# Moving ScalarE's copies of a turned layer step and of turned attention weights to other places of its row order

## The reference

```python
# layer 0
adj = adj + eye(N); d = sum(adj, -1) ** -0.5
out = (d[:, None] * adj * d[None, :]) @ x @ W.T + b
# layer 1
q, k = x @ WQ, x @ WK
h = relu(q[:, None, :, :] + k[:, :, None, :])          # for each pair (i, j)
score = einsum('bijd,d->bij', h, p)
out = softmax(score + where(adj > 0, 0, -1e22), -1) @ x
# layer 2 (degrees from |adj + eye|) and layer 3 (from adj)
out = (d[:, None] * adj * d[None, :]) @ x @ W + b
# after each layer
x = layernorm(x + out)
```

## Time and profile before

| | us |
|---|---|
| median of 3 runs | 14193.57 |
| lowest, highest | 14191.82, 14194.89 |
| the profiled execution's own time | 14193.55 |
| its span, first to last instruction | 14191.7 |
| PE busy | 13028.6 (92%) |
| VectorE busy | 13378.4 (94%) |
| ScalarE busy | 13088.8 (92%) |
| GpSimd busy | 908.8 (6%) |
| mean granted TensorE clock | 0.98 |

### The profile page before, as it was taken

The page is one execution under the profiler, slowest core; times in us unless marked ns, Lnnn a source line. Parts: engine busy times, 40 slices in busy tenths (PEclk is TensorE's granted clock), DMA queues, the critical chain, the costliest instruction groups (busy, mean ns, idle before and its releaser), DMA issues.

```text
span 14191.7 us, 317692 instructions
## 1 busy us (share of the span) xinstructions
PE 13028.6 (92%) x143877; PEld 5473.6 (39%) x143877; DVE 13378.4 (94%) x14048; ACT 13088.8 (92%) x8612; POOL 908.8 (6%) x615
## 2 busy tenths in 40 slices
PE   6889989999899998999989998899989999899988
PEld 3333334443344433443334433344333443333333
DVE  5999999999999999999999999999999999999995
ACT  5999899998999999998999989999899998998994
POOL 0000000000000000001000000000000010000000
PEclk8999999999999999999999999999999999999999
DMA  5111112221122111221122211222112221011103
GB/s 185 45 52 47 49 52 84 87 61 49 56 86 88 61 41 61 87 88 58 36 73 85 85 55 36 77 83 85 59 35 74 88 80 56 30 49 52 43 12 108
DMA packets 714329, 935.45 MB, mean 66 GB/s; under 512 B 61712, under 2 KB 455952, under 8 KB 693520
## 3 DMA queue, kind: packets, MB, share of 16 engines
q1 hardware_dynamic: 712976, 915.13, 20.6%
HBM read 722.01 MB, written 184.55 MB: 64 GB/s over the span
## 4 chain that ended last, share of the span: by engine, by line
PE 45%; DVE 31%; ACT 20%; issue 2%; DMA 2%; SPq 0%; POOL 0%; ACTq 0%; DVEq 0%; POOLq 0%
PE score L1165 33%; DVE big L1019 27%; ACT big L783 18%; PE acc L1086 6%; PE turn L1063 2%; PE acc L1145 2%; DVE att L968 1%; DVE gx L898 1%; DMA piece<-adj_turned 1%; DMA q_pair_kept<-turned 1%; PE acc L1104 1%; ACT y_turned L706 0%; ACT turned L696 0%; DVE stats L904 0%; DMA big<-in_adj_dram 0%
## 5 line engine op out<-in xcount | busy, mean ns | idle before, releaser
L1019 DVE TENSOR_SCALAR big<-q_pair,k_pair_cols 128x2048 f32<-128x2048 f32 x10120 | 12224.7, 1280 | 418.9 <-PE score L1165 400.1
L783 ACT ACTIVATE big<-q_f,k_cols 128x2048 f32<-128x2048 f32 x6144 | 11744.7, 1998 | 63.5 <-DMA q_f<-q_kept 43.3
L1165 PE MATMUL score<-big,sign_window 128*32 128x512 f32 x49152 | 5612.0, 597 | 291.4 <-ACT big L783 287.1
L1165 PE MATMUL score<-big,unit_window 128*32 128x512 f16 x81920 | 5186.5, 397 | 726.0 <-DVE big L1019 708.0
L1165 PEld LDWEIGHTS score<-big,unit_window 128*32 128x32 bf16 x81920 | 2285.8, 97 | 3897.8 <-issue 1110.4
L1165 PEld LDWEIGHTS score<-big,sign_window 128*32 128x32 f32 x49152 | 1565.3, 110 | 3624.9 <-issue 3002.2
L1086 PE MATMUL acc<-piece,gs 128*128 128x512 f32 x3072 | 1446.2, 598 | 34.8 <-DVE gs L881 22.4
L1086 PEld LDWEIGHTS acc<-piece,gs 128*128 128x128 f32 x3072 | 533.6, 191 | 544.6 <-issue 459.5
L607 POOL TENSOR_SCALAR att_var<-att_mom 128x1 f32<-128x1 f32 x128 | 66.2, 517 | 9806.9 <-DVE att_mom L986 9806.9
L764 ACT ACTIVATE att_turned<-turn 128x512 f32<-128x512 f32 x512 | 299.9, 586 | 346.2 <-PE turn L1063 346.0
L1145 PE MATMUL acc<-x,att_turned 128*128 128x128 f32 x4096 | 555.2, 279 | 0.0
(11 more groups left out here) (89 smaller groups left out, 2705.6 us busy)
## 6 DMA issues: line engine op xcount, KB each, us to landing
piece<-adj_turned SPq DMA_DIRECT2D x1536, 256.0 KB, 2.7
att<-in_adj_dram SPq DMA_DIRECT2D x128, 1024.0 KB, 5.2
raw<-in_adj_dram SPq DMA_DIRECT2D x224, 512.0 KB, 4.6
adj_turned<-turned SPq DMA_DIRECT2D x224, 512.0 KB, 4.3
big<-in_adj_dram SPq DMA_DIRECT2D x32, 512.0 KB, 7.5
adj_turned<-big SPq DMA_DIRECT2D x32, 512.0 KB, 6.9
gx<-in_x_dram SPq DMA_DIRECT2D x32, 256.0 KB, 4.4
q_kept<-raw SPq DMA_DIRECT2D x32, 256.0 KB, 3.7
```

The costliest lines, as they stand in the source:

```text
L783: ins = nc.scalar.activation(ring["A"][:, RANK[g] % RING * 4 + u, :], q_f32[:], ACT.Relu, bias=k_cols[:, t % 2, QUAD * u + g:QUAD * u + g ...
L1019: ins = nc.vector.tensor_scalar(ring["D"][:, RANK[g] % RING * 4 + u, :], q_pair[:], k_pair_cols[:, t % 2, QUAD * u + g:QUAD * u + g + 1], ...
L1165: ins = nc.tensor.matmul(score[QUAD * u:QUAD * (u + 1), cc, :], window[:, QUAD - 1 - g:2 * QUAD - 1 - g], row, start=(g == 0 and part == 0 ...
```

## The change

Two things move on ScalarE. The copy of a turned layer step goes from the side work of group 26 to that of group 28, which is ScalarE's work before the rows of group 29; it is then behind the rows of group 26 and behind the copy of a turned raw quarter at group 27. The constant TURNED_AT also enters the two places that work out which steps and passes lie before which others; no pass lies between 26 and 28. And the four copies of turned weights go from the start of groups 9, 13, 17 and 22, ahead of the side work there, to behind the first of the four rows of groups 10, 13, 18 and 23. The number of instructions, their shapes and all waits stay as they are.

```diff
-    SELF_AT, TURNED_AT, PROJECT_AT, SUM_AT, ROOT_AT, NORM_OUT_AT, STORE_AT = 18, 26, 28, 35, 36, 40, 41
+    SELF_AT, TURNED_AT, PROJECT_AT, SUM_AT, ROOT_AT, NORM_OUT_AT, STORE_AT = 18, 28, 28, 35, 36, 40, 41
...
-        COPY_AT = {9: 0, 13: 1, 17: 2, 22: 3}
+        COPY_IN = {10: 0, 13: 1, 18: 2, 23: 3}
...
-                    if before and g in COPY_AT:
-                        copy_weights(c * T + (T + t - 1), COPY_AT[g])
                     side(c, place)
                     if KIND[g] == "A":
...
                         for u in range(P // QUAD):
+                            if before and u == 1 and g in COPY_IN:
+                                copy_weights(c * T + (T + t - 1), COPY_IN[g])
                             ins = nc.scalar.activation(ring["A"][:, RANK[g] % RING * 4 + u, :], q_f32[:], ACT.Relu,
```

## The result

| us | kernel before | changed kernel |
|---|---|---|
| median | 14191.6 (12 runs) | 14158.08 (12 runs) |
| lowest, highest | 14181.26, 14204.43 | 14150.9, 14165.78 |
| profiled execution, its span | 14193.55, 14191.7 | 14165.78, 14164.0 |
| mean granted TensorE clock | 0.980 | 0.977 |

The ratio is 0.9976, with a 95% interval of 0.9967 to 0.9985: 33.5 us faster, where 34.2 had been forecast. The profiled execution of the changed kernel is the slowest of its 12.

The account below looks back on a forecast made before the run. TensorE, ScalarE and VectorE, passing work round a ring of two groups, were taken to bound the kernel together. 17.8 + 15.5 + 3.8 - 2.9 = 34.2 us off 14193.57 gave 14159.4, range 14136 to 14195.

Parts of the forecast that it names:

- Part 1, tied borders: Layer copy behind group 26: where VectorE's chain is only 0.60 us behind TensorE's, even-block borders gain 0.60 us before copy costs.
- borders 5 and 9: Behind blocks 5 and 9 VectorE is 1.0 and 1.3 us late by its own work: nothing to win.
- the whole stop: Rival: each of 84 borders gives TensorE's 1.13 us wait at group 26, 14099 us; chance 0.05.
- VectorE alone: Rival: VectorE alone sets the time, so the layer copy and queue give nothing, about 14195 us; chance 0.14.
- Part 2, what the copies cost: Weight copies inside groups: 0.48 us later from group 13, cutting some middle-batch border gains; +2.9 us in block 0.
- Block 0's 0.48: In block 0 of the six later batches ScalarE sets the pace from group 13; 0.48 us paid each, +2.9 us.
- No slower kernel from group 13: Denies the rival that ScalarE, late from group 13, paces blocks 3 to 8: 14218 or 14202 us; chance 0.09.
- the 0.2 named as the limit: Forecast is wrong if TensorE gets new waits before groups 13, 18 and 21 of more than 0.2 us.
- The stop of 0.20 us named for group 21 of block 6: With ScalarE's rows of group 21 later, TensorE is 0.20 us late there, and so is VectorE's group 27.
- A wait inside a group: Copies breaking up four like rows taken to cost nothing; if each of some 74 lost one overlap, 7 us worse.
- Part 3, the queue: Behind blocks 11 and 12 the query pair's store leaves 1.11 us sooner on SyncE's queue: 14 borders, 15.5 us.
- Odd blocks' wait at group 26: TensorE's wait for ScalarE's rows of group 26 would fall from 1.15 to about 0.9 us in odd blocks.

Follow-up runs that it names:

- corner 12: Changed kernel plus ten unused identity products on TensorE ahead of group 4's scores in blocks 3 to 13, holding its clock: 14090.64 us, ratio 0.9931.
- corner 9: Kernel before, neither copy moved, plus ten unused identity products ahead of group 4's scores in blocks 3 to 13: 14141.01 us, ratio 0.9967.
- corner 10: Kernel before with only the copies of turned weights moved, plus ten unused products ahead of group 4's scores in blocks 3 to 13: 14142.76 us, ratio 0.9968.
- run 6: Changed kernel with the second quarter's weight copy put back ahead of group 13's side work: 14162.26 us, ratio 0.998.
- 11: Kernel before with only the layer copy moved, plus ten unused products ahead of group 4's scores in blocks 3 to 13: 14092.83 us, ratio 0.9931.
- run 3: Changed kernel with the query pair's store on SyncE's queue at group 27 instead of 29, ahead of the piece loads: 14137.64 us, ratio 0.9961.

## Why the prediction came out, step by step

With the clock held the traces can be read border by border. Take the distance between TensorE's first scores of group 4 in one block and in the next, corner 12 less corner 9, mean of the six middle batches, against the steps of the forecast (us; the border is named by the block before it):

```
border      0     1     2     3     4     5     6     7     8     9    10    11    12    13    14    15
forecast  +.48    0   -.60  -.42  -.60    0   -.40  -.19  -.40    0   -.35 -1.11 -1.11    0     0     0
measured  +.47  -.39  -.50  -.47  -.59  +.01  -.45  -.19  -.48  -.03  -.36 -1.28 -1.32  -.53  +.14  -.38
spread     .05   .88   .31   .03   .08   .07   .05   .09   .03   .04   .11   .34   .59   .56   .69  1.07
```

The spread is the standard deviation over the six batches.

- **Part 1, tied borders.** Right, each within 0.10 us; borders 5 and 9, said to be VectorE's own, gave nothing. Neither the whole stop (-1.13 each) nor VectorE alone (0) fits this row of numbers. Forecast for the seven borders 2, 3, 4, 6, 7, 8 and 10: 2.96 a batch; measured 3.04.
- **Part 2, what the copies cost.** Block 0's 0.48 is there (+0.47; +0.46 in corner 10 alone). In corner 10 borders 3 to 8 are longer by 0.04 to 0.36; in the six middle batches all borders sum to +9.9 us, where about 8 followed from the forecast's steps. That the time does not show it lies outside these borders: in corner 10's profile the first and last batch are 5.2 us shorter together, and the scores begin 3.6 us earlier, in an opening without any such copy. Over the 12 profiles with the store at its old place that start varies by 6.5 us (237.6 to 244.1; 231.4 and 231.6 with the early store), so a single profile's opening proves nothing, and run 6, which took the largest of these costs away without a gain in time, leaves it open whether they reach the time.
- **No slower kernel from group 13.** Right: the new wait of TensorE in block 7 is 0.13 us at group 18, under the 0.2 named as the limit. The stop of 0.20 us named for group 21 of block 6 is recorded as no idle time, but TensorE's starts do shift by it: with the copies moved (corner 12 less 11) the scores behind group 21 come 0.22 us later, 0.07 of it at group 13.
- **A wait inside a group.** It cost no overlap: the row behind the copy at 7834.28 starts at 7834.75 (0.47 later), and the copy starts 1.90 behind the row before it. Over all 512 copies of the changed kernel the median of the first distance is 0.48 us, the same as before. ScalarE around block 6's group 10, changed kernel:

```profile
7832.38 2.01 ACT L783 ACTIVATE big<-q_f,k_cols 128x2048 f32<-128x2048 f32 x1
7834.28 0.59 ACT L764 ACTIVATE att_turned<-turn 128x512 f32<-128x512 f32 x1
7834.75 5.81 ACT L783 ACTIVATE big<-q_f,k_cols 128x2048 f32<-128x2048 f32 x3
```

- **Part 3, the queue.** Right in kind, low in size. VectorE arrives 1.33 us later in relation to TensorE's group 28 than before, not 1.11, and the store leaves 1.00 us behind that group's start in both. The mean of the 14 waits fell by 1.00 us in the first pair and by 1.34 with the clock held (2.11 to 0.78): 14 x 1.34 = 18.7 us against 15.5. From its issue until VectorE goes on the store takes 3.6 to 5.8 us, which is why single blocks, such as the one shown, can look unchanged.
- **Odd blocks' wait at group 26.** 0.58 to 0.68 us where I said about 0.9; where ScalarE gained the difference was not looked into.
- **The term that was missing.** Nothing in the sum stood for the clock. That the total hit to 0.7 us is partly luck: the change gave 50 us with the clock held, 16 more than the sum (borders 1, 11 to 13 and 15, 10 us over the six batches, the rest in the first and last batch and an opening 5.0 us shorter in that pair of profiles), and about 17 of them are not there with the clock free. Two misses of like size, one for and one against, cancel. The borders 1, 13 and 15 have spreads of 0.56 to 1.07, about as large as one slow group 4, and the products reach only groups 4 of blocks 3 to 13; whether their changes are the change's own stays open.
- **A slip without weight.** By its own terms the rival of VectorE alone is 14193.6 + 2.9 = 14196.5, not 14195.

## What to carry to other kernels

The list of waits said that ScalarE stood 523 us before one copy, and moving it removed 325 of them; the time fell by 33. What a wait is worth was read at each border as the distance to the next late engine, 0.2 to 0.6 us here out of 1.15 us of TensorE's wait. And when group after group of like products has one that takes longer, look at the granted clock before the sum is closed: a wait that an engine has anyway can be filled with useful products, and here three pieces moved into it were worth twice the change itself (67 us against 33.5).

## What was not expected of the hardware

- Behind a wait of 2.78 us TensorE's granted clock was 0.54 over the next scores, and 32 products took 3.38 instead of 2.0 us. It hit 61 of 96 blocks before and 63 after, and a wait as long did not always bring it: block 6 of batch 4 of the changed kernel, 2.80 us of wait, took 2.00. In 46 of the 63 the granted clock fell after the scores had begun.
- Ten unused 128x128 f32 products (2.50 us in the trace) in that wait took away all but 2, 1, 1 and 0 of the slow scores in corners 9 to 12, and the time fell by 46 us (before) and by about 62 (changed). Two products are recorded for each that the kernel names (x20 for ten).
- The flight of a like store, from issue until VectorE goes on, differed between 3.6 and 5.8 us within one execution. Issued 13.7 us earlier, ahead of three piece loads instead of behind them, it landed after 2.3 to 2.6 us (run 3).
